# Segment ends taken up beside the last expert units, 24 of 37 coefficient pieces made within the relation sums, and the edge's norm as the scale of a row copy

## The reference, cut to what matters

```
x = x + gnn0(LN(x))                                     # mean over incoming edges of (LN(x) W + b)
# L0 ffn: graph attention with 4 heads chooses 2 of 4 experts per node
h = x @ W_gat
e = leaky_relu(a_src[src] + a_dst[dst]); e_max = segment_max(e, dst)
alpha = exp(e - e_max[dst]) / (segment_sum(exp(e - e_max[dst]), dst)[dst] + 1e-16)
scores = mean_over_heads(layernorm(segment_sum(h[src] * alpha, dst) + b_gat))
x = x + sum over the top 2 of 4 experts of  w * (gelu(LN(x) @ W1 + b1) @ W2 + b2)
# L1 gnn: relations, 32 relations made of 8 bases, 50000 edges sorted by dst
weight = einsum('rb,bio->rio', w_comp, bases)
msg = einsum('ni,rio->nro', LN(x), weight)[src, rel_type] * norm
x = x + relu(segment_sum(msg, dst))
x = x + ffn1(LN(x))                                     # 8 experts, routed by the mean node, layernorm
```

## Time and profile before

| | |
|---|---|
| median of 3 runs | 2281.04 us (2280.89 to 2281.67) |
| the profiled execution | 2285.36 us |
| its span | 2283.6 us, mean granted clock of PE 0.851 of full speed |
| PE busy | 1666.2 us (73%), 8780 instructions |
| DVE busy | 1276.7 us (56%) |
| POOL busy | 1076.5 us (47%) |
| ACT busy | 712.2 us (31%) |
| row copies of the relation sums (L2111), 592 | 213.9 us, 408 ns each |
| gathers of the attention (L1490), 256 | 244.9 us, 957 ns each |
| second halves' copies to `ys` (L1843), 100 | 39.0 us, 419 ns each |

### The profile page before, as it was taken

How to read it: one execution, slowest core, us unless ns; L and a number is a source line. 1 busy time by engine, 2 the same in 40 slices (tenths; PEclk the granted TensorE clock), 3 DMA queues, 4 the chain that set the end, 5 groups by cost and what they waited for, 6 DMA issues and landing times. The chain is left out here.

```text
span 2283.6 us, 32653 instructions
## 1 busy us (share of the span) xinstructions
PE 1666.2 (73%) x8780; PEld 1319.3 (58%) x8781; DVE 1276.7 (56%) x3698; ACT 712.2 (31%) x1566; POOL 1076.5 (47%) x1102
## 2 busy tenths in 40 slices
PE   2776566766777799999934646565756799996997
PEld 1444344444445577777723546555645699984786
DVE  7877777667677410222146636555656566656235
ACT  1001146555651222222204632232323233312222
POOL 1676666555660566666640065555555554300000
PEclk9987578788789799999966867777777799997999
DMA  5233233333332122232251543433333565611001
GB/s 165 78 89 92 73 98 104 96 104 103 101 97 74 29 70 70 69 91 70 76 158 8 177 129 117 133 118 118 116 112 114 166 219 197 201 37 42 0 1 57
DMA packets 165026, 226.82 MB, mean 99 GB/s; under 512 B 35764, under 2 KB 124118, under 8 KB 162070
## 3 DMA queue, kind: packets, MB, share of 16 engines
q0 software_dynamic: 47392, 105.58, 16.5%
q1 hardware_dynamic: 114176, 115.99, 15.7%
q10 hardware_dynamic: 3318, 3.59, 0.5%
HBM read 172.48 MB, written 105.03 MB: 122 GB/s over the span
## 5 line engine op out<-in xcount | busy, mean ns | idle before, releaser
L473 POOL DMA_INDIRECT edge_rows<-xn_table,edge_source x391 | 376.5, 963 | 402.2 <-ACT held L2111 177.6
L2123 PE MATMUL part<-coef,held 128*128 128x128 f32 x2368 | 400.8, 317 | 215.7 <-issue 181.0
L473 POOL DMA_INDIRECT shared_space<-xn_table,edge_source x391 | 402.4, 1029 | 277.8 <-issue 108.5
L2123 PEld LDWEIGHTS part<-coef,held 128*128 128x128 f32 x2368 | 371.4, 228 | 254.6 <-issue 199.3
L2161 DVE SCALAR_TENSOR_TENSOR window_sums<-window_sums,fine_keep,part 128x256 f32 x592 | 282.4, 477 | 295.9 <-remote 130.2
L763 PE MATMUL part<-shared_space,hot 128*128 x832 | 297.9, 495 | 123.9 <-issue 63.4
L2111 ACT ACTIVATE held<-edge_rows 128x256 f32 x592 | 213.9, 408 | 484.6 <-PE part L2123 228.3
L1490 POOL DMA_INDIRECT gall<-attention_table,attention_source x256 | 244.9, 957 | 132.5 <-issue 68.3
L763 PEld LDWEIGHTS part<-shared_space,hot 128*128 128x128 f32 x832 | 176.7, 239 | 194.2 <-issue 173.4
L1148 DVE TENSOR_TENSOR shared_space<-shared_space,part 128x257 f32 x416 | 174.6, 420 | 132.8 <-remote 43.5
L2148 DVE SCALAR_TENSOR_TENSOR coef<-iota,fine_target,slot_coefs 128x128 f32<-128x128 f32 x592 | 203.7, 346 | 6.8 <-PEq L1283 6.8
(11 more groups left out here) (467 smaller groups left out, 1926.4 us busy)
## 6 DMA issues: line engine op xcount, KB each, us to landing
basis_sums<-window_sums SPq DMA_DIRECT2D x74, 1024.0 KB
z<-basis_sums SPq DMA_DIRECT2D x21, 1024.0 KB
expert_rows<-ys SPq DMA_DIRECT2D x20, 640.0 KB
shared_space<-expert_rows SPq DMA_DIRECT2D x25, 512.0 KB, 4.7
W<-in_L_ffn_W SPq DMA_DIRECT2D x20, 512.0 KB
gall<-attention_digits SPq DMA_DIRECT2D x32, 256.0 KB
xn_table<-shared_space SPq DMA_DIRECT2D x10, 640.0 KB, 4.1
shared_space<-xn_table,edge_source POOLq DMA_INDIRECT x391
```

The source lines that it names most:

```text
L473: pool.indirect_dma_start(rows[:, b % ring, 0:D], None, table, bass.IndirectOffsetOnAxis(ap=esrc[:, b:b + 1].bitcast(U32), axis=0)).then_i ...
L2123: mm = nc.tensor.matmul(part[n][:, c * P:(c + 1) * P], held[n][:, c * P:(c + 1) * P], coef[n][:, :, :].rearrange("p b w -> p (b w)"), star ...
```

## The change

- `Mixing` is a new class that holds what a coefficient piece needs (the relations as bf16, the norm, the numbers to compare with, the identity, the parts of w_comp, five semaphores) through both stages, and has its three shared steps: `compare`, `turn`, `products`.
- `experts_before` goes from 5i/8 halves to 9i/16. `AFTER_UNIT` goes to 6, 11, 15, 17: the last segment piece now stands behind the first copy of unit 17's results, with the last column's copies right behind it. PE's four small carry matmuls stand before `down(19)`, VectorE's scans over the lanes before unit 19's copies. ScalarE's exponents for the last piece stand inside unit 19, after its fourth gelu. POOL has a new wait for all first matmuls of units 0 to 18 before the gathers of the segment ends, since `ended` now lies in the first W1 tile.
- The first 13 pieces (`RS_EARLY`) are made where all 37 were. The other 24 are made in the steps 0 to 51 of the relation sums, one every two steps: comparison at step i, transposes at i + 2, ScalarE's copy at i + 3, products at i + 4, ScalarE's copy into `coefs` at i + 5. VectorE waits for a piece before it makes weights from it.
- `coefs` is made without the norm. ScalarE's row copy multiplies by it instead, as a scale from a tile, one value per partition.
- The ring of rows of the first stage has 40 blocks instead of 44, and several small tiles lie elsewhere.

The diff, cut to its core:

```diff
+RS_EARLY = 13
...
+RING_A, RING_T = 40, 32
...
+class Mixing:
+
+
+    def __init__(self, sb, sem):
+        self.relb, self.norm = sb("slot_relb", [P, KT], BF16), sb("slot_norm", [P, KT])
+        self.relation, self.ident = sb("relation", [P, RELS, QT], BF16), sb("identb", [P, P], BF16)
+        self.parts = sb("wcomp_parts", [P, 3, QT * BASES], BF16)
+        self.hot_ready, self.turned, self.copied, self.ready, self.made = (
+            sem(n) for n in ("relhot_ready", "relt_ready", "relt_copied", "coef_ready", "coefs_made"))
+
+    def compare(self, V, hot, i):
+        return V.tensor_tensor(hot, self.relb[:, i * RQ:(i + 1) * RQ].rearrange("p (g q) -> p g q", q=QT).unsqueeze(2)
+                               .to_broadcast([P, RQ // QT, RELS, QT]), self.relation[:, :, :].unsqueeze(1).to_broadcast([P, RQ // QT, RELS, QT]),
+                               ALU.is_equal)
+
+    def turn(self, nc, to, hot):
+        for q in range(RQ // QT):
+            mm = nc.tensor.transpose(to[:, q * P:(q + 1) * P], hot[:, q, :, :].rearrange("p r q -> p (r q)"), self.ident[:, :])
+        return mm
+
+    def products(self, nc, to, hot_t):
+        for q in range(RQ // QT):
+            for n in range(3):
+                mm = nc.tensor.matmul(to[:, q * QT * BASES:(q + 1) * QT * BASES], hot_t[:, q, :], self.parts[:, n, :],
+                                      start=(n == 0), stop=(n == 2))
+        return mm
...
-AFTER_UNIT = [8, 14, 18, 19]
+AFTER_UNIT = [6, 11, 15, 17]
...
-    half, part = divmod(5 * i, 8)
+    half, part = divmod(9 * i, 16)
...
-        return kind, done * per + per * part // 8
+        return kind, done * per + per * part // 16
...
+        ended = free[:, 0:NT * EW].rearrange("p (t w) -> p t w", w=EW)
...
+        crossed = done[:, 0:NT * EW].rearrange("p (t w) -> p t w", w=EW)
...
+            pool.wait_ge(h_ready, (UNITS - 1) * 2 * FC)
...
+                    if m == UNITS - 1 and n == FC - 1:
+                        exponents(PIECES - 1)
+                for c in range(PIECES - 1):
+                    if AFTER_UNIT[c] + 2 == m:
...
-            down(UNITS - 1)
-
+
+            pe.wait_ge(h_used, UNITS * 2 * FC)
...
+            down(UNITS - 1)
...
+            pe.wait_ge(y_used, UNITS * CT)
             turn_relations(0)
-            for i in range(RS):
-                if i + 1 < RS:
+            for i in range(RS_EARLY):
+                if i + 1 < RS_EARLY:
                     turn_relations(i + 1)
-                pe.wait_ge(relt_copied, i + 1)
+                pe.wait_ge(mix.copied, i + 1)
                 if i > 1:
-                    pe.wait_ge(coefs_made, i - 1)
-                for q in range(RQ // QT):
-                    for n in range(3):
-                        mm = nc.tensor.matmul(coef_ps[i % 2][:, q * QT * BASES:(q + 1) * QT * BASES], relhot_t[i % 2][:, q, :],
-                                              wparts[:, n, :], start=(n == 0), stop=(n == 2))
-                mm.then_inc(coef_ready, 1)
+                    pe.wait_ge(mix.made, i - 1)
+                mix.products(nc, coef_ps[i % 2], relhot_t[i % 2]).then_inc(mix.ready, 1)
...
+                if m == UNITS - 1:
+                    carry_lanes()
...
+                        if c == PIECES - 1:
+                            for _ in parts:
+                                pass
+                            lane_ends()
...
+                dve.wait_ge(mix.ready, i + 1)
+                V.tensor_copy(coefs[:, i * RQ:(i + 1) * RQ, :], coef_ps[i % 2].rearrange("p (t b) -> p t b", b=BASES)).then_inc(mix.made, 1)
...
+def coefs_at(i, lag):
+
+    n, odd = divmod(i - lag, 2)
+    return RS_EARLY + n if not odd and 0 <= n < RS - RS_EARLY else None
+
+
+assert 2 * (RS - RS_EARLY - 1) + 5 < USED
...
-                                         ACT.Copy).then_inc(copied, 1)
+                                         ACT.Copy, scale=mix.norm[:, k:k + 1]).then_inc(copied, 1)
+                    p = coefs_at(i, 3)
+                    if p is not None and n == 6:
+                        act.wait_ge(mix.turned, p + 1)
+                        nc.scalar.activation(relhot_t[:, :, :].rearrange("p q e -> p (q e)"), relt_ps, ACT.Copy).then_inc(mix.copied, 1)
+                    p = coefs_at(i, 5)
+                    if p is not None and n == 6:
+                        act.wait_ge(mix.ready, p + 1)
+                        nc.scalar.activation(coefs[:, p * RQ:(p + 1) * RQ, :], coef_ps.rearrange("p (t b) -> p t b", b=BASES),
+                                             ACT.Copy).then_inc(mix.made, 1)
...
+                p = coefs_at(i, 4)
+                if p is not None and q == 1:
+                    pe.wait_ge(mix.copied, p + 1)
+                    pe.wait_ge(mix.made, p)
+                    mix.products(nc, coef_ps, relhot_t).then_inc(mix.ready, 1)
+                p = coefs_at(i, 2)
+                if p is not None and q == 1:
+                    pe.wait_ge(mix.hot_ready, p + 1)
+                    pe.wait_ge(mix.copied, p)
+                    mix.turn(nc, relt_ps, relhot).then_inc(mix.turned, 1)
...
+                        if (k + DEEP) % RQ == 0:
+                            dve.wait_ge(mix.made, (k + DEEP) // RQ + 1)
                         weights(k + DEEP)
+                    p = coefs_at(i, 0)
+                    if p is not None and n == 2:
+                        dve.wait_ge(mix.turned, p)
+                        mix.compare(V, relhot[:, :, :, :], p).then_inc(mix.hot_ready, 1)
```

More of the change, by code:

```diff
@@ L1254, in __init__ @@
         self.gall = sb("gall", [P, GT, GW])
-        self.rel, self.norm = sb("slot_rel", [P, KT]), sb("slot_norm", [P, KT])
+        self.rel, self.norm = sb("slot_rel", [P, KT]), norm
         self.htab, self.pay = sb("htab", [P, NT, GW]), sb("target_pay", [P, NT, PW])
@@ L1343, in attention_and_experts @@
         done = hid[0][:, :, :].rearrange("p f n -> p (f n)")
-        ended, crossed = (done[:, n * NT * EW:(n + 1) * NT * EW].rearrange("p (t w) -> p t w", w=EW) for n in range(2))
-        done = done[:, 2 * NT * EW:]
+        crossed = done[:, 0:NT * EW].rearrange("p (t w) -> p t w", w=EW)
+        done = done[:, NT * EW:]
         acc, sq = (done[:, n * NT * C16:(n + 1) * NT * C16].rearrange("p (t k) -> p t k", k=C16) for n in range(2))
@@ L1771, in _ @@
             for n in range(3):
-                link(V.tensor_copy(wparts[:, n, :], left))
+                link(V.tensor_copy(mix.parts[:, n, :], left))
                 if n < 2:
-                    link(V.tensor_tensor(wrest, left, wparts[:, n, :], ALU.subtract))
+                    link(V.tensor_tensor(wrest, left, mix.parts[:, n, :], ALU.subtract))
                     left = wrest
@@ L2130, in _ @@
                         if t == 0:
+                            pe.wait_ge(mix.made, RS)
                             pe.wait_ge(third.w_in, 16 * 5)
@@ L2192, in _, with third_update @@
             link.wait()
-def third_update(nc, common, a, X, iota, ident, ones, third, out):
+def third_update(nc, common, a, X, iota, ident, ones, mix, third, out):
     var_ready, std_ready = common.var_ready, common.std_ready
@@ L2221, in third_update @@
         b1, b2 = sb("b1_6", [P, K2, FC]), sb("b2_6", [P, K2, D])
-        bias = sb("bias6", [P, D])
+        bias = mix.norm[:, 0:D]
         z_ps = pb("z_ps", [P, 2, 512])
```

133 lines of the change are left out of this document (62 added, 71 removed).

## The result

The changed kernel takes 2298.71 us (median of four runs, 2297.47 to 2301.28) against 2280.97 (2280.55 to 2281.67) for the kernel before on the same chip: a ratio of 1.0065, 95% interval 1.0050 to 1.0081, thus 17.7 us slower. The profiled execution took 2298.33 us with a span of 2296.6, 13.0 more than the span of before. The forecast was 2292.

A forecast was written before the change was run, and what follows sets the result against it. It took PE to bound the experts, busy 308.4 of 323.6 us, and the relation sums with products at 99%, with late signals beside POOL's gathers. +35 - 48 + 24 = +11 on 2281.04 gave 2292 us, range 2250 to 2320.

The forecast's parts named there:

- Term 1: Experts: the faster pace of gathers lengthens POOL's bursts and PE loses more in them, +35 us, bounds 0 to +50.
- theory of late signals: Beside POOL's gathers: after some 8 us without a break, other engines see PE's finished work late and PE runs out of banks.
- my model of 16.7 us of work in each burst: Experts: 16.7 us of PE work admit 3.4 groups of gathers, the burst grows to 3.7 groups, 5.8 us a group.
- Term 2: End of unit 17 to the segment ends: earlier ends and 24 fewer pieces there, -48 us, bounds -58 to -38.
- Term 3: Relation sums without basis products: 24 coefficient pieces at 1.0 us each, +24 us, bounds 0 to +50.
- rival C: Relation sums: ScalarE's longer row copy is not hidden and delays POOL's restart, +16, worst case +55, named 2308 us; chance 0.10.
- The norm as a scale: Relation sums: ScalarE's row copy gets some 0.1 us longer, to 0.50 to 0.51, costed at nothing because VectorE hides it.
- The ring at nothing: First stage: 40 instead of 44 rows cost nothing, since the lead of 16 blocks holds POOL first.
- The sum: Whole kernel: +35 - 48 + 24 = +11 us, added to the median of 2281.04.
- Rival A: Experts: no longer bursts, or late signals stay as they are; first term 0, 2245 to 2262 us, middle 2257; chance 0.34.

The follow-up runs named there:

- crossed_first: Changed kernel with the load of the crossed sums ahead of the first twelve loads of expert rows: 2003.24 us, ratio 0.9952 against the kernel before, second kind of chip.
- after_third: The changed kernel once more, unaltered, on a chip of the first kind: 2294.71 us, ratio 1.0049 against the kernel before.
- no_scale: Changed kernel with a plain row copy in the relation sums, the norm left out: 2297.13 us, ratio 1.0049 against the kernel before.
- all_early: Changed kernel with all 37 coefficient pieces made before the relation sums, the norm still in the row copy: 2299.49 us, ratio 1.0053 against the kernel before.
- after_again: The changed kernel once more, unaltered, on a chip of the second kind: 2010.31 us, ratio 0.9983 against the kernel before.
- bursts_of_16: Kernel before, waiting for the experts only before every fourth group of gathers: ratio 1.0000 on the second kind; repeated as bursts_of_16_b on the first kind, 1.0333.
- ring40: Kernel before with 40 rows instead of 44 in the first stage's ring, nothing else: ratio 0.9997 against the kernel before.
- two runs of late pieces: Changed kernel with pace, segment pieces and carry put back, leaving 24 pieces in the relation sums and the norm as scale: ratios 1.0006 and 1.0001, second kind.

## Why the prediction came out as it did

The direction and the range were right. The mechanisms of the first two terms held in the main, that of the third did not, and the forecast lies as near as it does partly because errors of both signs met. Point by point:

- **Term 1, +35.** Measured 36.1 in the changed kernel, 35.3 with the pace alone, and 39 to 42 in the later traces of the changed kernel and its variants on the first kind (404.2 to 407.3 against 365.1). The theory of late signals made a strong forecast, that 16 gathers in a row at the old mean pace cost 15 to 30 us, and on the first kind it was 72 us in the experts (437.5 against 365.1), more than twice of it, where the rival said none: the direction is borne out, the price of a longer burst was sized too low. Three parts of my working were rough, so that 35 came out this near is luck in part. The 36 us are not all standing: 15.8 are PE's matmuls at a lower granted clock, which my model of 16.7 us of work in each burst did not have. The bursts are not of 12 and 16 in turn: if every break over 0.5 us ends one, there are 30, most of 4, 8 and 12, with two of 16 and one of 20, against 28 before, 13 of them of 12. Longer bursts show only if breaks up to 1.5 us are not counted: then there are 20 against 23, the longest of 28 gathers against 16. And my model had POOL's last gather at 1140 to 1150; it starts at 1157.5.
- **Term 2, -48.** Measured -40.4, up to the instruction that needs the crossed sums. VectorE was to start on the ends 62 us after the end of unit 17. Its first instruction there did, at +63.5; the second had to wait for the crossed sums, until +73.6, and that wait is what the term missed. POOL began at +14.7 (I had 16). The last copy to `ys` came at +43 instead of +36, the twelve loads were issued from +46.5 in 18.1 us instead of 14.4, and the load of the crossed sums landed 9 us after its issue, for which I had 2. The prediction named the crossed sums behind the expert rows as what is late next; on the second kind of chip that wait is 3.95 us, and crossed_first removes it. The 13 early pieces were done at +63.6.
- **Term 3, +24.** This is the mis-sized term: 9.1 us in the first trace, 10.1 in after_third (700.8) if set against the mean of the four traces of the old relation sums on the first kind, 690.7 (688.4 to 694.1). The time is lost where the term had it: the stretch without products, from the first row copy to the first product, takes 495.1 and 491.5 us, in those four traces 480.5 to 485.5. But its attribution failed: the step "1.0 us a piece, the row copy at nothing" would give +24 for the pieces without the scale, and no_scale shows 690.6; the scale alone in all_early shows 691.6. Only both together have the 10 us, as far as one execution of each of these two runs tells, on another chip than the two traces with both. POOL's gaps of over 3 us between bursts in the stretch without products add up to 124.5 and 122.5 us in the two traces with both, and to 104.5 in before, 95.1 in no_scale and 111.8 in all_early. That fits the mechanism of rival C, in which POOL restarts when ScalarE has caught up with a row of copies, with ScalarE's copies for the pieces among them. That it is so was not shown, and each figure is one execution's.
- **The norm as a scale.** 0.500 us instead of 0.416, as in the forecast's 0.50 to 0.51. It adds 84 ns between these medians, 93 between the shortest copies (491 against 398), and 94 between the medians on the second kind (494 in after_again against 400 in bursts_of_16). The Trainium skill, "ScalarE: Activation LUTs", section "What ACT_TABLE_LOAD costs", gives 93 ns for each such pointer operand, and the traces agree. The longer copy stays hidden as long as nothing else is added to ScalarE: all_early has it, and 691.6 us.
- **The ring at nothing.** ring40 bears it out. The 6 us by which the experts started later had no part in the sum; single executions differ by 14 us there.
- **The sum.** 36.1 - 40.4 + 9.1 is +5, where I had +11; the profile has 13.0, of which 6.2 and 1.6 lie where nothing was forecast, and ring40 and after_third give the 6.2 to single executions. Term 3 was 15 too high, term 2 8 too low, and these two met. The median's 17.7 is larger by 4.7, since the profiled execution of before was 4.3 above its own median and that of after was not; on the chip of after_third the difference of the medians is 12.1, next to the forecast's 11.
- **Rival A** (no longer bursts, or late signals that stay as they are) is wrong on the first kind, and right on the second, where the time falls, though by 3 us and not by 24: the experts hardly change with the pace (331.1 against 329.0 and 329.3 in the two runs of late pieces, with the old pace), the later stretch gains 7.7 (64.6 against 72.3 in bursts_of_16), and the relation sums lose 3.4 of it (587.3 against 583.9).

## What to carry to other kernels

Transfers that GpSimd issues without a break can delay the signals by which other engines see TensorE's results, and the price grows with the length of the burst: on the first kind of chip the experts take 365 us with bursts mostly of 12, 400 with a slightly faster pace and 437.5 with 16 gathers in a row, on the second kind 329 to 331 whatever the pace. So a pace is not only a mean rate. And what it costs differs with the chip: a change that trades a faster pace for an earlier end lost 0.65% on one and won 0.17% on another, so that one chip's result should not decide it.

Work taken out of a stretch brings nothing where a chain beside it is as long (24 pieces, 18 us, 1 us gained on the second kind). And two small additions that are each hidden may not be hidden together.

## What the runs showed of the hardware that I had not expected

- The kernel before takes 2281 to 2287 us on three chips and 2013 on two, with the same instructions. The difference lies in the stages beside GpSimd's gathers, as bursts_of_16 shows, the nearest to the kernel before that has a trace on the second kind: the experts start at 672 instead of 766 to 780, take 329 instead of 365 to 368, the relation sums 584 instead of 691, and the last stage, without gathers, takes 266 to 268 on both. A gather takes the same 0.94 us plus 0.30 on both. The idle time before ScalarE's gelu and its releasers, bursts_of_16_b and then bursts_of_16:

```profile
L1532 ACT ACTIVATE hid<-ps_of_attention,b 128x320 f32<-128x320 f32 x160 | 81.9, 527 | 327.6 <-remote 158.7 <-PE ps_of_attention L1636 130.9 <-issue 38.0
```

```profile
L1532 ACT ACTIVATE hid<-ps_of_attention,b 128x320 f32<-128x320 f32 x160 | 84.3, 527 | 223.3 <-PE ps_of_attention L1636 223.2
```

  158.7 us marked remote against none. The program is the same in both; what in the chips makes the difference, the runs do not tell.
- TensorE's stalls cost twice. In the experts on the first kind, without their first 33 us, the granted clock is 0.98 before, 0.93 with the faster pace and 0.91 with bursts of 16 (on the second kind, where PE does not stand, 1.00), and with the 0.93 came 15.8 us of longer matmuls in the changed kernel beside 20.4 of standing.
